# The causal mask of two-head maximum tiles: added by TensorE, followed by one plain maximum on VectorE

## What is computed

```python
xn = _layernorm(x)
q, k, v = heads(xn @ w_qkv.T + b_qkv)             # 32 heads of 16, scores scaled by 1/sqrt(16)
scores = einsum('bqhd,bkhd->bhqk', q, k) * scale + slopes[:, None, None] * positions
scores = where(q_pos >= k_pos, scores, -1e9)
attn = softmax(scores)                            # its row maximum is what the change is about
s = einsum('bhqk,bkhd->bqhd', attn, v) @ w_out.T + b_out
out = x + s * silu(ffn(xn))
```

## Time and profile before

| | |
|---|---|
| median of 3 runs | 889.02 us (886.86 to 889.53) |
| profiled execution | 884.88 us, its span 883.0 us |
| mean granted clock of TensorE | 0.986 of full |
| busy in the span | PE 815.3 us (92%), PEld 354.8 (40%), DVE 639.5 (72%), ACT 471.4 (53%), POOL 120.5 (14%) |
| L1137, fused masked maximum | 512 instructions, 221.9 us busy |
| L1141, plain maximum | 256 instructions, 158.4 us busy |
| L1423, matmuls of the maximum tiles | 768 instructions, 195.0 us busy |

### The profile page before, as it was taken

The page is one execution under the profiler, slowest core; times in us unless marked ns, Lnnn a source line. Parts: engine busy times, 40 slices in busy tenths (PEclk is TensorE's granted clock), DMA queues, the critical chain, the costliest instruction groups (busy, mean ns, idle before and its releaser), DMA issues.

```text
span 883.0 us, 16119 instructions
## 1 busy us (share of the span) xinstructions
PE 815.3 (92%) x5938; PEld 354.8 (40%) x5938; DVE 639.5 (72%) x1818; ACT 471.4 (53%) x615; POOL 120.5 (14%) x136
## 2 busy tenths in 40 slices
PE   5799989999999999999899999999999899998997
PEld 4345434444444434334333333333333333333333
DVE  5375786743433555664799999999999999996556
ACT  4443265333132222222378887877788788778540
POOL 3123131323032122122000000000000005500000
PEclk9999998999999999999799999999999999999999
DMA  7735321248401100100111222221215223543645
GB/s 219 215 108 173 126 84 72 96 116 254 165 1 71 72 1 25 71 1 25 72 44 56 65 75 76 64 75 52 65 55 168 82 74 114 183 128 122 187 150 204
DMA packets 72591, 88.40 MB, mean 100 GB/s; under 512 B 26926, under 2 KB 39214, under 8 KB 72000
## 3 DMA queue, kind: packets, MB, share of 16 engines
q1 hardware_dynamic: 72384, 87.10, 31.1%
q0 software_dynamic: 128, 0.27, 0.2%
HBM read 51.15 MB, written 35.93 MB: 99 GB/s over the span
## 4 chain that ended last, share of the span: by engine, by line
PE 68%; DVE 17%; issue 7%; DMA 5%; ACT 2%; SPq 0%; POOL 0%; ACTq 0%; DVEq 0%
PE psum L1463 13%; PE psum L1423 9%; PE psum L1486 9%; PE psum L1487 9%; DVE mshown L1137 5%; PE psum L1497 4%; DVE mx L1141 4%; PE psum L1498 4%; PE psum L1439 4%; PE psum L1323 2%; PE psum L1325 2%; PE psum L1324 2%; PE psum L1337 2%; PE psum L1335 2%; PE psum L1336 2%
## 5 line engine op out<-in xcount | busy, mean ns | idle before, releaser
L869 ACT ACTIVATE probs<-psum,exp_scale 128x1024 f32<-128x1024 f32 (+1 forms) x320 | 312.7, 1027 | 93.6 <-PE psum L1448 56.5
L1137 DVE CUSTOM_DVE_ANT_0 mshown<-psum,ahead 128x384 bf16<-128x384 f32 (+3 forms) x512 | 221.9, 487 | 14.9 <-PE psum L1423 13.7
L1423 PE MATMUL psum<-QKs 51*128 51x512 f16 (+3 forms) x768 | 195.0, 333 | 18.4 <-DVE mx L1137 7.3
L1463 PE MATMUL psum<-probs,Vs 128*32 128x512 f32 (+3 forms) x1536 | 162.1, 510 | 16.4 <-ACT osum L875 16.2
L1141 DVE TENSOR_REDUCE mx<-psum 128x1 f32<-128x512 f32 x256 | 158.4, 682 | 2.7 <-PE psum L1423 1.7
L1439 PE MATMUL psum<-QKs 53*128 53x512 f16 (+3 forms) x768 | 139.9, 331 | 2.2 <-DMA QKs<-mrows 1.6
L1486 PE MATMUL psum<-X,room 128*128 128x512 f16 (+1 forms) x352 | 133.9, 380 | 0.0
L1487 PE MATMUL psum<-X,room 128*128 128x512 f16 (+1 forms) x352 | 133.4, 379 | 0.0
L1423 PEld LDWEIGHTS psum<-QKs 51*128 51x128 f16 x768 | 53.2, 94 | 169.0 <-DVE mx L1137 88.9
L894 ACT ACTIVATE room<-psum,gate_half 128x512 f32<-128x512 f32 (+1 forms) x44 | 30.2, 687 | 109.9 <-PE psum L1487 109.9
L1171 DVE SCALAR_TENSOR_TENSOR room<-room,psum 128x512 f32<-128x512 f32 (+1 forms) x44 | 30.2, 687 | 67.6 <-ACT room L894 67.6
(11 more groups left out here) (158 smaller groups left out, 911.6 us busy)
## 6 DMA issues: line engine op xcount, KB each, us to landing
o_scr<-osum SPq DMA_DIRECT2D x32, 256.0 KB, 2.4
QKs<-q_scr SPq DMA_DIRECT2D x96, 64.0 KB
QKs<-k_scr SPq DMA_DIRECT2D x96, 64.0 KB
q_scr<-qk_stage SPq DMA_DIRECT2D x16, 256.0 KB, 2.2
k_scr<-qk_stage SPq DMA_DIRECT2D x16, 256.0 KB, 2.2
v_scr<-v_stage SPq DMA_DIRECT2D x16, 256.0 KB, 2.0
Vs<-v_scr SPq DMA_DIRECT2D x16, 256.0 KB
probs<-in_L_attn_x SPq DMA_DIRECT2D x4, 1024.0 KB, 11.4
```

Source lines behind the costliest of these rows:

```text
L869: nc.scalar.activation(probs[n % PSLOTS][:, 2 * pair:2 * pair + 2, 0:COLS[n]], s_bank[pair][:, :, 0:COLS[n]], ACT.Exp, scale=exp_scale[:, ...
L1137: last = nc.vector.tensor_tensor_reduce(out=mshown[at % 2][:, cols], in0=m_bank[bank][:, cols], in1=ahead[:, CH - keys:], scale=1.0, scala ...
L1423: last = nc.tensor.matmul(tile[:, hh, :], Qs[s][rows, pair + hh, qb * P:(qb + 1) * P], Ks[s][rows, pair + hh, k0:k0 + keys], start=(hh == ...
L1463: last = nc.tensor.matmul(pv_bank[32 * h:32 * h + 32, CH - cols:CH], Vs[s][:, kb, h::QH], probs[n % PSLOTS][:, h, at:at + cols], start=(kb ...
```

## The change

Masked tiles with two heads are treated in another way; masked tiles with one head and unmasked tiles stay as they are. In `fill_max`, two matmuls are added behind the two of such a tile. For r = 0 and 1, `unit[half, r]` is the weight (64 rows of the tile's own half x 128), and `causal[half, r]`, repeated for both heads, is the moving operand: 2 x 128 = 256 columns, the last 128 keys of each head. They accumulate on the tile, and the signal `max_filled` goes with the second. In `read_max`, such a tile then goes to the plain `tensor_reduce` over both heads at once, as unmasked tiles do; the two fused instructions, their scratch output and their waits are gone. For a masked tile with one head, the loop over heads with one turn is written as one instruction.

```diff
@@ read_max
-                if masked_tile(qb, k0, keys):
+                if n == 1 and masked_tile(qb, k0, keys):
                     dve.wait_ge(s_const, CONSTS)
                     dve.wait_ge(max_read, at - 1 + MRING)
-                    for hh in range(n):
-                        cols = slice(hh * keys, (hh + 1) * keys)
-                        last = nc.vector.tensor_tensor_reduce(out=mshown[at % 2][:, cols], in0=m_bank[bank][:, cols], in1=ahead[:, CH - keys:], scale=1.0,
-                                                              scalar=LOWEST, op0=ALU.add, op1=ALU.max, accum_out=dst[:, hh, :])
-                    last.then_inc(max_read, 1)
+                    nc.vector.tensor_tensor_reduce(out=mshown[at % 2][:, 0:keys], in0=m_bank[bank][:, 0:keys], in1=ahead[:, CH - keys:], scale=1.0,
+                                                   scalar=LOWEST, op0=ALU.add, op1=ALU.max, accum_out=dst.rearrange("p h q -> p (h q)")
+                                                   ).then_inc(max_read, 1)
                     return
                 nc.vector.tensor_reduce(dst, m_bank[bank][:, 0:n * keys].rearrange("p (n k) -> p n k", n=n), AX.X, ALU.max
                                         ).then_inc(max_read, 1)
@@ fill_max
-                rows = slice(u * HALF, u * HALF + ROWS_MAX)
+                masked = masked_tile(qb, k0, keys) and n > 1
+                rows, half = slice(u * HALF, u * HALF + ROWS_MAX), slice(u * HALF, (u + 1) * HALF)
                 tile = m_bank[bank][:, 0:n * keys].rearrange("p (n k) -> p n k", n=n)
                 for hh in range(n):
                     last = nc.tensor.matmul(tile[:, hh, :], Qs[s][rows, pair + hh, qb * P:(qb + 1) * P], Ks[s][rows, pair + hh, k0:k0 + keys],
-                                            start=(hh == 0), stop=(hh == n - 1))
+                                            start=(hh == 0), stop=not masked and hh == n - 1)
+                if masked:
+                    for r in range(2):
+                        last = nc.tensor.matmul(tile[:, :, keys - P:], unit[half, r], causal[half, r].unsqueeze(1).to_broadcast([HALF, n, P]),
+                                                start=False, stop=(r == 1))
                 last.then_inc(max_filled, 1)
```

## The result

The changed kernel takes 894.61 us (median of 7 runs, 891.9 to 897.22) against 888.72 us before (7 runs, 884.74 to 891.21). The ratio is 1.0085, with a 95% interval of 1.0061 to 1.011: slower, by 0.6 to 1.1%. The forecast was 898.6 us, in a range of 889.5 to 904.5. The profiled execution has a span of 891.4 us, 8.4 more than the one before.

What follows compares the result with a forecast made beforehand. TensorE was taken to bound the feed-forward stage, a chain through TensorE, ScalarE and VectorE the attention groups. Terms 2.4 + 3.3 + 3.9 = +9.6 us gave 894.5 profiled, 898.6 us as median; range 889.5 to 904.5.

Steps and rivals of the forecast that it cites:

- What bounds the kernel: TensorE in the feed-forward stage; in attention, VectorE and TensorE alternating, then a chain without VectorE; period 25.30 us.
- the signs that were to show it: Profile after: period 25.8 us, feed-forward 2.4 longer, shorter copy wait, new VectorE idle before items 1, 3 and row transpose.
- What VectorE saves: Attention groups: 0.085 us on each of three 2x128 tiles, 0.07 on each of four 2x256; 0.54 per group.
- Feed-forward stage, +2.4: All of quad 0 and items 0 to 3 of quad 1: 11 pairs at 0.22 us, nothing overlapping.
- the third rival: At every mask pair, the array changes over between row counts: about 16 us more, 914; chance 0.05.
- End of a group, +3.3: Items 29, 32, 33 of 15 groups: item 29's pair costs 0.22 us each time, the other two are free.
- Start of a group, +3.9: Items 0 to 3 of 14 groups: TensorE's added matmuls make VectorE 0.28 us late in each.
- The walk: Step-by-step delays from item 0 to the row transpose at a group's start, ending with VectorE 0.28 us late.
- the pairs of items 1 and 2 stand in line ahead of the scores and item 3: +0.37: Group start: these pairs delay scores and item 3 by 0.37 us, the rest overlapping; item 3 ready 0.70 later.
- my bound for no overlap at all: Upper bound at a group's start: four pairs, 0.85 us, less 0.12 slack, so +0.73 a group.
- Sum: Whole kernel: 2.4 + 3.3 + 3.9 = +9.6 us, 898.6 us in terms of the median, 1.1% slower.
- The first (VectorE bound, pairs riding in the other half): Attention: VectorE stays the bound, 0.31 us saved a group; 887.1 us, or 890.4 with item 29's pair; chance 0.20.

Runs made afterwards that it cites:

- the mask added twice: Against the changed kernel: VectorE keeps the two fused reads for two-head masked tiles while TensorE also adds the mask; 895.83 us, 1.0092 of before.
- The two-pair kernel: Against the changed kernel: the pair of mask matmuls is issued twice for each two-head masked tile; 910.13 us, 1.0239 of before.

## Why the prediction was right, point by point

**What bounds the kernel.** Right. TensorE in the feed-forward stage, and in attention a chain through TensorE, ScalarE and VectorE with its weak point at item 29 and the copy of the output bank. Removing one pair there, or moving the order, changed the period by what the rows had said. Of the signs that were to show it, the wait for the copy is there and shorter (1.05), but the period is 25.48 and not 25.8, and VectorE has new idle time ahead of item 1 alone (0.17), none ahead of item 3 or the row transpose.

**What VectorE saves.** Right in size (0.34 and 0.60 for the two plain forms, where 0.345 and 0.62 were taken), and right in that most of it is hidden: 0.17 of 0.54 us is worth something.

**Feed-forward stage, +2.4.** Measured 250.0 - 247.6 = 2.4. The pair follows its tile directly; from the changed kernel's trace:

```profile
301.51 0.39 PE L1422 MATMUL psum<-QKs 51*128 51x256 f16 x2
301.74 0.38 PE L1426 MATMUL psum<-causal,unit 64*128 64x256 bf16 x2
302.06 0.39 PE L1489 MATMUL psum<-X,room 128*128 128x512 f16 x1
```

It is 0.55 from the tile to the next matmul, 0.32 before: 0.23 for the pair. A further changeover between 51 and 64 rows, the third rival, is not there: the mask starts 0.23 after the tile, about as long as the tile's own 512 columns take (0.22 in the earlier trace rows). In the kernel before, a 64-row mask starts 0.22 after the 53-row scores of 512 columns in its half (605.48 and 605.26). So neither 51 and 64 nor 53 and 64 rows show a changeover between them here.

**End of a group, +3.3.** Measured 0.23 for each of 15 groups, 3.4. Items 32 and 33 were free, as said: the periods with them (25.25) and without (25.25 to 25.26) are the same.

**Start of a group, +3.9.** This term was mis-sized: it is -0.04 in a group, -0.6 us, where I had +0.28. The walk was right down to item 1: the product step came 0.12 late (0.11 forecast), item 1 was taken 0.13 late (0.11). It failed at "the pairs of items 1 and 2 stand in line ahead of the scores and item 3: +0.37". TensorE in the changed kernel, items 1 to 4:

```profile
608.18 1.09 PE L1466 MATMUL psum<-probs,Vs 128*32 128x512 f32 x8
...
609.21 0.29 PE L1422 MATMUL psum<-QKs 51*128 51x128 f16 x3
609.33 0.27 PE L1426 MATMUL psum<-causal,unit 64*128 64x256 bf16 x1
609.35 0.27 PE L1422 MATMUL psum<-QKs 51*128 51x256 f16 x1
609.45 0.28 PE L1426 MATMUL psum<-causal,unit 64*128 64x256 bf16 x2
609.56 0.38 PE L1442 MATMUL psum<-QKs 53*128 53x512 f16 x1
...
610.01 0.27 PE L1422 MATMUL psum<-QKs 51*128 51x256 f16 x1
...
610.23 0.27 PE L1426 MATMUL psum<-causal,unit 64*128 64x256 bf16 x1
610.24 0.33 PE L1422 MATMUL psum<-QKs 51*128 51x384 f16 x1
...
610.53 1.09 PE L1466 MATMUL psum<-probs,Vs 128*32 128x512 f32 x8
```

and before, the scores behind item 1, and the end of VectorE's read of item 0:

```profile
605.26 0.38 PE L1439 MATMUL psum<-QKs 53*128 53x512 f16 x1
...
605.67 0.08 DVE L1137 DVE_READ_ACCUMULATOR2_ANT mx<- 128x1 f32 x1
```

That last row is where the fused read ends: in the kernel before, one such record, 84 ns in the mean, stands behind each of the 512 CUSTOM_DVE_ANT_0 of L1137 and writes the maximum to `mx`.

Item 1 (rows 64 to 127) and item 2 (rows 0 to 63) run side by side from their first matmuls on. The first row holds three matmuls, two of item 1 and one of item 2, and item 2's starts at 609.23, ahead of item 1's second (609.28), which stands before it in the program. Their pairs then lie beside each other, and so do item 3's pair and item 4's tile (610.23 and 610.24). I had let the issue order serialise them more than it does. From item 1 to the scores behind it it is now 0.35 us, 0.12 before, so the two pairs cost about 0.22 together, the length of one, where I had 0.37.

Item 3 started at 610.01, 5.49 after the restart against 5.25 before, so 0.24 late and not 0.48. The 0.12 of the product step and the 0.22 of the pairs make 0.34; the other 0.10 was slack that I had not seen. Before, item 3 started at 605.82, some 0.06 behind the end of VectorE's read of item 0, whose bank it takes; TensorE could have come 0.10 earlier. With the mask added twice, where that read of item 0 lies as it did before, item 3 still starts 5.49 after the restart: TensorE's own work holds it there, and not the bank. Item 3's own pair then fell into item 4's old wait of 0.31. The product step behind it was 0.08 late (6.01 against 5.93) instead of 0.39, and the row transpose as well. Before, the transpose had been ready 0.12 ahead of VectorE's copy, so 0.08 does not delay the copy, and VectorE's relief brings it forward until it starts as soon as the transpose is ready: it comes 7.34 after the restart, where it is 7.51 with the mask added twice. The two-pair kernel shows how near that was: one pair more for each tile and the start is 0.74 longer, as much as my bound for no overlap at all.

**Sum.** Two terms right, one wrong by 4.5 us; the sum of what was shown is 5.1 us of 9.6. The median moved by 5.9, and the ratio stands for 7.5 (5.4 to 9.8). The group behind the last maxima, longer by 1.8 on average, brings the sum to 6.9. That group was no term of mine, and that it made good part of the 4.5 is luck. The forecast median was 4.0 us too long.

**Rivals.** The first (VectorE bound, pairs riding in the other half) is nearer than my forecast for the start of a group and holds nowhere else; even there only 0.04 of its 0.31 came. The price of item 29 that spoke against it decided. I had given too little to a mixture of it and the forecast.

## What to carry to other kernels

When work is moved between engines, price it at the places of the order where it lands, not by the engines' busy shares: of seven equal pairs in an attention group, one lengthened the period by its full 0.23 us, and the other six cost 0.12 between them, which VectorE's relief made good, while in the feed-forward stage each was paid. Where two halves of TensorE's array are in use, look for what runs in the other half at that place: the pairs of items 1 and 2, which lie beside each other, cost what one costs (0.22 us together), while a pair ahead of matmuls over all rows was paid in full (0.23), and of a second helping 0.74 of 0.88 us was paid. And the chain that shows such a place also shows the better remedy: putting the product step and the scores ahead of the maxima they were queued behind gave 0.38 us in a group in the kernel before and 0.61 in the changed one, where the change confined to items 0 to 3 gives 0.05.

## What the runs showed of the hardware

A matmul on rows 0 to 63 of the array (609.23) started between two on rows 64 to 127 (609.21 and 609.28) that both stand before it in the program, and a mask on one half and a tile's matmul on the other started at 609.33 and 609.35: here the halves kept separate time. Within one half, matmuls of 256 columns started 0.11 us apart. And at one place of the program, where TensorE stands idle for 1.39 to 2.85 us, the granted clock of the next 4 us was low (0.57 to 0.68) in seven of fourteen profiles: in all six with an idle of 2.03 us or more and in one with 1.78, while idles of 1.81 to 1.98 left it at 1.00. What decides was not found. Between two profiles of the changed kernel, the first with the low clock and the second at 1.00, this group differs by 2.1 us (35.06 and 32.96), of which the longer wait is 0.55; by that estimate the low stretch costs some 1.5 us.
